# Four layers of attention and feed-forward: stacked scores in the small attention, attentions pipelined by one head, rounded copies on ScalarE

## The reference

```python
x = x + L0_xattn(layernorm(x), ctx, mask, position_bias, ...)   # 32 heads of 128, own k and v per head
x = x + L0_ffn(layernorm(x), ...)          # silu(h1) * h3, low-rank additions, 1376 hidden
x = x + L1_xattn(layernorm(x), ctx, mask1, ...)   # the small attention
x = x + L1_ffn(layernorm(x), ...)          # one of every 32 hidden units, picked by argmax
x = x + L2_xattn(layernorm(x), ctx, ...)   # 32 query heads, 8 key/value heads, q and k rms-normed
x = x + L2_ffn(layernorm(x), ...)          # top 2 of 8 low-rank experts on one base product
x = x + L3_xattn(layernorm(x), ctx, ...)   # 32 query heads, 8 key/value heads, biases
x = x + L3_ffn(layernorm(x), ...)          # gelu, 2048 hidden
```

```python
q, k, val = (einsum('ed,bdw->bew', W, patches) + b)    # 64 channels: 8 heads of 8
scores = einsum('bhdi,bhdj->bhij', qh, kh) / sqrt(8)
scores = where(mask > 0, scores, -1e9)
o = gelu(einsum('bhij,bhdj->bhdi', softmax(scores), vh))
out = (einsum('de,bew->bdw', Wo, o) + bo) * masks
```

## Time and profile before

| | |
|---|---|
| median of the runs | 3458.11 us (3456.35 to 3464.62) |
| the profiled execution | 3458.61 us |
| its span in the profile | 3456.7 us |
| TensorE products | 3137.7 us busy, 91%, 15840 of them |
| VectorE | 1975.3 us, 57%, 3823 instructions |
| GpSimd | 1141.7 us, 33%, 935 |
| ScalarE | 943.9 us, 27%, 3176 |

### The profile page before, as it was taken

How to read it: one execution, slowest core, us unless ns; L and a number is a source line. 1 busy time by engine, 2 the same in 40 slices (tenths; PEclk the granted TensorE clock), 3 DMA queues, 4 the chain that set the end, 5 groups by cost and what they waited for, 6 DMA issues and landing times.

```text
span 3456.7 us, 47231 instructions
## 1 busy us (share of the span) xinstructions
PE 3137.7 (91%) x15840; PEld 2524.9 (73%) x15840; DVE 1975.3 (57%) x3823; ACT 943.9 (27%) x3176; POOL 1141.7 (33%) x935
## 2 busy tenths in 40 slices
PE   5999999999989889989989888888878999999899
PEld 4778888888768644457767677777766888888687
DVE  7555555555543454477766666666666444445643
ACT  2222222222210033310033333333322333333211
POOL 4333333433255222136621221222113322232264
PEclk9999999999999965579999999999989999999999
DMA  2111111111111000021110110110002111111011
GB/s 97 40 40 42 36 39 45 45 42 36 44 43 39 18 20 13 7 60 31 41 34 19 28 30 18 30 30 24 9 22 58 29 35 30 30 38 29 26 51 46
DMA packets 68604, 120.64 MB, mean 35 GB/s; under 512 B 7840, under 2 KB 13216, under 8 KB 68112
## 3 DMA queue, kind: packets, MB, share of 16 engines
q1 hardware_dynamic: 68496, 119.23, 11.6%
HBM read 117.11 MB, written 2.10 MB: 34 GB/s over the span
## 4 chain that ended last, share of the span: by engine, by line
PE 71%; DVE 17%; issue 6%; ACT 3%; POOL 2%; DVEq 0%; DMA 0%; POOLq 0%; ACTq 0%; SPq 0%
PE proj L341 31%; PE outp L341 18%; PE heado L823 5%; PE score L803 4%; PE score L1593 3%; PE turn L816 2%; DVE nw_t L370 2%; PE score L341 2%; DVE nw_t L368 1%; DVE tbuf L988 1%; PE turn L742 1%; ACT sq L897 1%; DVE x L1038 1%; DVE rowmax L993 1%; DVE stats L390 1%
## 5 line engine op out<-in xcount | busy, mean ns | idle before, releaser
L341 PE MATMUL outp<-w_out,acts 128*128 128x512 f32 x3288 | 867.8, 408 | 38.0 <-DVE x L1038 20.0
L341 PE MATMUL proj<-xnT,w_in 128*128 128x512 f32 x3288 | 783.5, 393 | 9.5 <-DVE big L864 3.0
L341 PEld LDWEIGHTS outp<-w_out,acts 128*128 128x128 f32 x3288 | 607.8, 193 | 176.3 <-DVE x L1038 29.4
L341 PEld LDWEIGHTS proj<-xnT,w_in 128*128 128x128 f32 x3288 | 613.8, 189 | 141.7 <-issue 6.3
L341 PE MATMUL proj<-ctxT,w_kv 128*128 128x512 f32 x2304 | 563.4, 404 | 52.9 <-DVE big L864 43.7
L341 PEld LDWEIGHTS proj<-ctxT,w_kv 128*128 128x128 f32 x2304 | 443.0, 194 | 153.6 <-DVE big L864 46.6
L602 POOL TENSOR_TENSOR w_out<-ring,consts 128x512 fp32r<-128x512 f32 x96 | 104.0, 1083 | 1039.8 <-PE outp L341 1039.8
L1038 DVE TENSOR_TENSOR x<-x,outp 128x512 f32<-128x512 f32 x384 | 261.4, 686 | 255.6 <-PE outp L341 254.1
L913 ACT ACTIVATE pbuf<-tbuf,negmax 128x128 f32<-128x128 f32 x512 | 199.2, 390 | 396.9 <-DVE negmax L995 393.9
L602 POOL TENSOR_TENSOR w_kv<-ring,consts 128x512 fp32r<-128x512 f32 x96 | 105.8, 1102 | 465.0 <-DMA ring<-in_L_wk 465.0
L864 DVE COPY big<-proj 128x512 f32<-128x512 f32 x136 | 94.0, 691 | 255.7 <-PE proj L341 255.3
(11 more groups left out here) (239 smaller groups left out, 4032.7 us busy)
## 6 DMA issues: line engine op xcount, KB each, us to landing
ring<-in_L_wq SPq DMA_DIRECT2D x96, 256.0 KB, 2.7
ring<-in_L_wo SPq DMA_DIRECT2D x96, 256.0 KB, 2.6
ring<-in_F_in SPq DMA_DIRECT2D x52, 256.0 KB, 2.6
ring<-in_L_wk SPq DMA_DIRECT2D x48, 256.0 KB, 2.7
ring<-in_L_wv SPq DMA_DIRECT2D x48, 256.0 KB, 2.8
ring<-in_F_out SPq DMA_DIRECT2D x41, 256.0 KB, 2.6
ring<-in_mask SPq DMA_DIRECT2D x16, 256.0 KB, 3.2
x<-in_x SPq DMA_DIRECT2D x2, 1024.0 KB, 7.4
```

The source lines that it names most:

```text
L341: mm = pe.matmul(bank_ap, w_ap(a, c), rhs(b, c), start=first and c == 0 and n == 0, stop=last and c == chunks - 1 and n == len(PASSES) - 1)
```

## The change

It has three parts.

**Attentions one head ahead.** A step of head j now makes scores, maxima and exponentials of head j+1 (`scored`), and projects what head j+2 needs (`needed`, which replaces `needed_next`). Probabilities alternate between the two buffers `tbuf` and `pbuf`. The tables of tiles have a piece ahead (`OWN_FIRST`, `SHARED_FIRST`) and offsets of a group: weights are loaded and split two heads ahead. In LA[2] and LA[3] the keys of the next group are projected at the second or third head, the values at the fourth; the diagonals are spread at the third. VectorE's order in a step: scores of the next head, copies of projections, spread keys, adds and low parts, normalisation of the next head, roots. In LA[0] and LA[2] the maximum is negated in the reduction itself (`negate=True`), and the small instruction L995 goes.

**Small attention rebuilt.** ScalarE repeats the projection weights three times (96 rows: two halves of four heads apart), so that queries and keys come out as stacks whose products give high by high, low and high parts in one fp32r product of 98 rows, two of them carrying the mask. GpSimd makes the matrix of blocks for each unit (98 x 512) and the keys' low part, ScalarE the high parts, VectorE the masked keys and the queries' low part. Values are padded to 128 columns: eight of a head, zeros, and ones in rows 64 and up, so that all eight heads of a patch gather in one bank and the row sums stand in its lower half. The subtraction goes: the exponential reads the scores with the negative maximum as bias, in four pieces. Once per batch VectorE takes the reciprocal of 64 x 512 sums and multiplies. Biases sit in a bias operand and in an extra row of Wo, the output mask is multiplied on GpSimd. The transposes back (L1572, L1618) go. The loads and splits of F1 no longer wait for the last add of L1.

**Feed-forwards.** The high parts of weight tiles and of hidden activations move from GpSimd (L1167, L1188) to ScalarE.

```diff
     def tile(self, g, j, what):
 
-        return self.tiles * g + self.order.index((what, j))
...
+    SHARED_FIRST = [("k", 0, 0), ("v", 0, 0), ("q", 0, 0), ("q", 0, 1)]
+    SHARED_TILES = [("q", 0, 2), ("o", 0, 0), ("q", 0, 3), ("o", 0, 1), ("k", 1, 0), ("q", 1, 0), ("o", 0, 2), ("q", 1, 1),
+                    ("v", 1, 0), ("o", 0, 3)]
...
+        def needed(A, g, j):
+            h1, h2 = after(g, j), after(*after(g, j))
+            over = is_last_group(g) and j >= GH - 2
...
+            found = [] if over else [(*h2, "q")]
+            if is_last_group(g):
+                return found
+            if A.normed:
+                return found + ([(g + 1, 0, "k")] if j == 1 else [(g + 1, 0, "v")] if j == GH - 1 else [])
+            return [(g + 1, 0, "k")] + found if j == 2 else found + ([(g + 1, 0, "v")] if j == GH - 1 else [])
...
             def step(g, j):
...
-                new = needed_next(A, g, j)
-                spreads = A.normed and j == GH - 1 and new
-                for half in range(2):
-                    scores(g, j, half)
-                for n in new[:1]:
-                    take_projection(dve, False, A, *n)
-                normalise(g, j, 0)
...
+                ahead = scored(g, j)
+                for half in range(2) if ahead else ():
+                    scores(*ahead, half)
+                for n in needed(A, g, j):
+                    take_projection(dve, False, A, *n)
...
                 add_at(0)
                 for half in range(2):
                     add_at(1 + half)
...
+                for half in range(2) if ahead else ():
+                    normalise(*ahead, half)
                 add_at(3)
...
+                if A.layer != 3:
+                    dve.tensor_reduce(negmax[:, half, 0:BH], src, AX.X, ALU.max, negate=True).then_inc(m["negmax"], 1)
+                    return
```

```diff
         def l1_pe(pe):
...
+                pe.matmul(score[s][:, :], qstk[0:ROWS, b % 2, s, n * P:(n + 1) * P], kbd[0:ROWS, u % UNITS, :],
+                          start=True, stop=True).then_inc(m["sfull"], 1)
...
+                for h in range(4):
+                    e = (4 * s + h) * P
+                    mm = pe.matmul(sum1[b % 2][:, n * P:(n + 1) * P], v1[:, b % 2, n, e:e + P],
+                                   ptbuf[:, s, h * P:(h + 1) * P], start=s == 0 and h == 0, stop=s == 1 and h == 3)
...
+            for u in range(UNITS * B):
+                scores(u)
+                extras(u // UNITS, u % UNITS)
+                if u >= 2:
+                    turn_probabilities(u - 2)
+                if u >= 3:
+                    values(u - 3)
...
         def l1_dve(dve):
...
+            def normalise(b):
+                dve.wait_ge(m["av"], UNITS * (b + 1))
+                wait(dve, m["onorm"], b)
+                dve.reciprocal(inv1, sum1[b % 2][E1:2 * E1, :]).then_inc(m["inverted"], 1)
+                dve.wait_ge(m["inverted"], b + 1)
+                dve.tensor_tensor(o1[b], sum1[b % 2][0:E1, :], inv1, ALU.mult).then_inc(m["onorm"], 1)
+
+            def extras(b, i):
+                if i == 3 and b:
+                    normalise(b - 1)
+                if b + 1 < B:
+                    if i < 2:
+                        take_keys(b + 1, i)
+                    elif i in (4, 5):
+                        low_of_queries(b + 1, i - 4)
+                    elif i == 6:
+                        take_values(b + 1)
...
         def ffn_act(act, A):
...
+                    for what in A.what[:-1] if more else ():
+                        ffn_act_high(act, A, *after(g, j), what)
...
-            sp.wait_ge(L1["out_full"], B)
-            sp.wait_ge(L1["out_biased"], B)
             ffn_sp(sp, F1)
```

More of the change, by code:

```diff
@@ L1487, in l1_sp, with diagonal_blocks @@
+        def diagonal_blocks(k, first):
+            wide = spread1[:, k * 4 * H1 * P:(k + 1) * 4 * H1 * P].rearrange("p (n e) -> p n e", n=PATCH)
+            return [wide[:, :, h * (P + DH1) + first:h * (P + DH1) + first + DH1] for h in range(H1)]
         def l1_sp(sp):
@@ L1526, in l1_pool @@
-            in_pairs(pool, batch)
+            F0.events.wait(pool, "sfull", 2 * F0.chunks)
+            for k in range(2):
+                pool.memset(v1[:, k, :, :], 0.0).then_inc(m["padded"], 1)
+                pool.wait_ge(m["padded"], 2 * k + 1)
+                for block in diagonal_blocks(k, E1):
+                    one = pool.memset(block, 1.0)
+                one.then_inc(m["padded"], 1)
+            F0.events.wait(pool, "outfull", B * ((F0.chunks + 1) // 2))
+            pool.wait_ge(m["padded"], 4)
```

931 lines of the change are left out of this document (498 added, 433 removed).

## The result

The changed kernel takes 3329.55 us (median; 3325.88 to 3329.78), the kernel before beside it 3457.75: a ratio of 0.962, 95% interval 0.961 to 0.964. That is 7.6 us above the forecast of 3322 and inside its range. The profiled execution took 3325.88 us, span 3324.1, the fastest of the four. All times of stages and groups, here and in the experiments, are of the one profiled execution of a kernel; times of a whole kernel are medians.

The account below looks back on a forecast made before the run. TensorE was taken as the bound, busy 3137.7 of 3456.7 us; savings of 64 + 14 + 12 + 12 + 28 + 7 = 137 us from 3458.6 gave 3322 us, range 3230 to 3412.

Parts of the forecast that it names:

- the small attention's mechanism: Small attention loop: reciprocal delays the value projection, 3.4 us idle, then 7.3 us at half rate; batch 23.4 us.
- near 0.75: Small attention loop: the granted clock expected as a sign that the forecast holds.
- the rival with the low clock throughout: Small attention: the low clock lasts through the loop, 268 us, kernel 3400 us; chance 0.17.
- the third layer's minus 28: Third layer's attention: one head ahead cuts idle and low clock by 3.5 us per group, 28 us in all.
- Splits come in bursts of four tiles: Third layer's attention: GpSimd's bursts, 9.5 us each, still catch a root twice a group.
- After the first burst the root is done 8.8 us after the next head's start: Third layer's attention: the add then comes at 14.0 us, wanted at 10.3, leaving 3.7 us idle.
- the 96 to 101: Third layer's attention: group time in us expected as a sign; below 92 would prove the forecast wrong.
- Fourth layer: Fourth layer's attention: 1.5 of 1.8 us of waits per group go, minus 12 us, besides the last head's 4.
- First feed-forward: First feed-forward: copies moved to ScalarE lie beside TensorE's products, which set the pace; 0 us.
- Second: Second feed-forward: VectorE's low parts no longer slowed by GpSimd's copies, minus 7 us over 14 chunks.
- Tail: Small attention's tail and next stage: fewer VectorE instructions, less waiting for weight tiles and a shorter root, minus 14 us.
- the largest term: Small attention's loop: minus 64 us, the gain coming from the clock.

Follow-up runs that it names:

- e3: Changed kernel with GpSimd waiting, in the third layer's attention, for the step's roots ahead of each of a group's two bursts of splits; 3266.7 us.
- e5: As e3 on the changed kernel, but GpSimd's burst in a group's second head waits for the diagonals too; 3240.7 us.
- e7: Changed kernel with the negative of the maximum again its own instruction in the first and third layers' attentions; 3350.3 us.
- e10: Kernel before with only the maximum negated in the reduction in the first and third layers; 3452.9 us against 3458.5, ratio 0.999.
- e6: Changed kernel with the high parts of the feed-forwards' weight tiles and activations back on GpSimd; 3336.15 us.
- e2: Changed kernel with the small attention's reciprocal cut into four quarters, one behind each of four units' maxima; 3314.05 us.
- e8: Changed kernel with e5's waits, output products ahead of the spreading, and e2's quarters now behind the queries' low parts; 3199.8 us, ratio to the kernel before 0.927.
- e9: Kernel before with only GpSimd's wait for the roots ahead of both bursts in the third layer's attention; 3408.3 us against 3458.5, ratio 0.986.

## Why the prediction was right, and where not

**Right: the small attention's mechanism.** Idle 3.67 us (forecast 3.4), half rate for 6.6 (7.3), a batch 23.9 (23.4, between value projections at 1258.68 and 1282.56). The clock was 0.88; the forecast's "near 0.75" does not follow from its own terms, as 7.3 us at half rate in 23.4 give 0.84. The reciprocal took 3.36 us, not 4.2: the line through 4 and 8 columns was too steep, 512 columns cost 6.6 ns each. By the estimate from the Trainium skill's repeat count (VectorE: DVE Perf Modes, "First, the fixed hardware budget") it would have been 4.3; the measurement decides. The loop took 181.6 instead of 190 because eight batches were counted alike: the first has no reciprocal in it, the last no projections (value projections at 1214.04, 1236.04, 1258.68: 22.0 and 22.6 us).

**Right: the rival with the low clock throughout fell.** The mixture got its clock back within 7 us, as the earlier trace rows had suggested.

**Wrong: the third layer's minus 28.** The step that failed is "Splits come in bursts of four tiles", with what the forecast worked out from it: "After the first burst the root is done 8.8 us after the next head's start", and the diagonals at 10.9 after the second. Both chains were longer. The burst behind the fourth head has five tiles, not four (1972.10 to 1983.98), the root was done 10.7 us after the head's start, and the add came 16.1 us after the head's start, not 14.0: 5.5 us of wait, not 3.7. In the third head a fifth tile follows the four (to 1929.91) and catches the key's root; the diagonals were done 13.3 us after the head's start (1932.03 less 1918.69), not 10.9: 7.4 us at the spreading, not 5.2. The squares cost 2.2, not 1.2; the other heads 1.2 together, not 3.0. Sum 16.2 of idle, not 13, and 6.2 for the low clock: 22.4 us, what a group had before, and 102.4 a group, outside the 96 to 101 that were to show the forecast right. The cause named in the forecast, small instructions stretched by bursts, was right: e3 and e5 take 10.3 and 15.3 us per group away by moving the bursts alone, the latter in the fastest of six executions. Without the negated maximum the pipelined stage takes 838.6 us (e7), 14.4 more than before the change: what the pipelining brought here was a loss.

**Wrong: the negated maximum had no term.** The forecast named L995 nowhere in its sum. e7 puts it at 20.7 us, 16.6 of them in the third layer and 5.9 in the first, by the profiled execution; e10 at 14.6 in the third layer alone, though at 5.6 by the medians of the whole. It is all that kept that stage level.

**Sizes off.** Fourth layer: 3.0 us per group (76.6 to 73.6), not 1.5. The waits account for 1.8; the rest was not traced. The seven intervals between groups are 19.6 us shorter together (the first only 1.3) and the rest of the stage 7.9, 27.5 for 16. First feed-forward: forecast 0, measured 8.7, and e6 gives up to 6.3 of it back, so the copies on ScalarE shorten it; why, was not traced. Second: 11.8 for 7, and 10.5 of it return in e6. Tail: 7.7 for 14. The forecast let the copies move without a price here; e6 puts it at 5.8 us, GpSimd's order around the masks, and with them back on GpSimd the tail is 13.5 shorter than before. First layer, 4 us forecast: the last head's wait did go, from 4.88 to 0.96 us, but TensorE's waits for ScalarE's copy of the projections, 9.2 of it in one wait, grew from 6.8 to 10.5, and the stage stayed level.

**The sum.** By stages the forecast was missed by 41 us one way (30 of them the third layer) and by 37 the other. That the total came within 7.6 us is luck; the largest term alone was off by 10.

## What to carry to other kernels

Small VectorE instructions in a chain that TensorE waits for must not meet a burst of GpSimd's, when their operands lie in the on-chip buffer: a wait that shifts the burst by a few us costs nothing where the tiles have slack, and brought 62.8 and 88.9 us here. A head of slack by pipelining does not cure such a chain, as it runs once a head in any order; look first at what stretches it. The small attention's wait of 3.67 us was paid about twice, by itself and by the 3.3 us that the half rate behind it lost; with waits of at most 1.7 us (e2, e8) the loop's clock was 0.96 and 0.99, so here several short waits were better than one long. A copy that moves from one engine to another also moves that engine's order: look at what now stands ahead of the work that TensorE waits for, as in the tail.

## What the runs showed of the hardware that had not been expected

The stage of the experts takes 56.6 to 58.2 us or 67.5, with the same instructions. Stretches of that stage in the changed kernel and in e3:

```profile
2457.46:2514.09 56.63, 45.13 (x240) 36.27 (x241) 40.42 (x95) 6.94 (x17) 9.19 (x8) 0.94 0.17 47
```

```profile
2393.75:2461.25 67.50, 58.38 (x240) 48.99 (x241) 40.39 (x98) 7.04 (x17) 9.20 (x8) 0.75 0.14 39
```

In e3, e9 and e10 the clock stays at its low level with TensorE busy most of the time. In e3 (the row ends with 79 of 96 products):

```profile
2408.22 17.10 PE L382 MATMUL proj<-w_in,xnT 128*128 128x136 f32 x79
```

These are 0.216 us each, and all 96 of them take 20.73 us; in the changed kernel the same 96 take 11.44, 0.119 each. In e3 the low level lasts from 2404.90 to past 2428.75, some 24 us. Both had a wait of 6 to 8 us ahead (7.55 in the changed kernel, 6.18 in e3). e3's four executions come in two pairs, 3260.9 and 3262.4, 3271.1 (the profiled one) and 3272.9 us, so the two lengths may well be two outcomes of one kernel. What decides between them stays open; it is worth 10.5 us, more than 0.3% of the kernel, and must be taken out by stages before a small edit elsewhere is judged.
